# Attention of eight sequences on one core: from two loops of four sequences to one unrolled stream of 128 units, with the shares applied to the weighed values

## The reference

```python
x = x + _L0(x, cond, ...)          # gated recurrence
x = x + _L1(x, cond, ...)          # h = tanh(x Wx + b + h Wh)
x = x + _L2(x, cond, ...)
q, k, v = split(x @ c_attn_w + c_attn_b, 3)
k = concat([cond @ uk_w.T + uk_b, k]);  v = concat([cond @ uv_w.T + uv_b, v])
scores = q k^T / sqrt(32);  scores = where(kj <= qi + 1, scores, -10000.) + mask
out = softmax(scores) @ v
x = x + (out @ c_proj_w + c_proj_b)
```

## Time and profile before

| | |
|---|---|
| median of 3 runs | 4201.73 us (4198.7 to 4204.33) |
| the profiled execution | 4198.98 us, span 4197.3 us |
| recurrences and setup | to 3027.3 us of the span |
| attention loop | 3027.3 to 4197.3 us |
| TensorE busy over the span | 93% |
| VectorE, ScalarE, GpSimd busy | 59%, 25%, 3% |

### The profile page before, as it was taken

One profiled execution on the slowest core, in us unless ns is written; L12 is line 12 of the kernel. 1 busy time (PEld: TensorE's weight loads), 2 busy tenths in 40 slices (PEclk: granted clock), 3 DMA queues, 4 the chain that ended last, 5 costly groups with the idle time before them and its releaser, 6 DMA issues. The chain is left out here.

```text
span 4197.3 us, 167926 instructions
## 1 busy us (share of the span) xinstructions
PE 3891.2 (93%) x75946; PEld 2493.0 (59%) x75946; DVE 2455.8 (59%) x9312; ACT 1057.7 (25%) x3796; POOL 126.9 (3%) x137
## 2 busy tenths in 40 slices
PE   6799999999999999999999999997689888888988
PEld 5577777777666666666666667754444444444444
DVE  3565665665566556566656656653375667557565
ACT  1121111111111111111111111110053454345444
POOL 0000000000000000000000000000000000000000
PEclk9999999999999999999999999999799999999999
DMA  5000000000000000000000000010000000000000
GB/s 182 3 4 4 3 4 3 3 4 3 4 3 3 4 3 3 4 3 3 3 4 3 3 3 3 3 50 15 1 1 11 11 1 11 11 11 1 11 11 11
DMA packets 16600, 44.53 MB, mean 11 GB/s; under 512 B 1474, under 2 KB 1522, under 8 KB 15876
## 3 DMA queue, kind: packets, MB, share of 16 engines
q1 hardware_dynamic: 13572, 27.33, 1.8%
q10 hardware_dynamic: 2304, 6.29, 0.4%
HBM read 25.23 MB, written 8.39 MB: 8 GB/s over the span
## 5 line engine op out<-in xcount | busy, mean ns | idle before, releaser
L181 PE MATMUL bank<-wh,h 128*8 128x256 f32 x16384 | 983.8, 381 | 62.0 <-DVE h L356 31.4
L201 PE MATMUL bank<-wh,h 128*16 128x256 f32 (+1 forms) x17408 | 991.7, 369 | 52.8 <-ACT h L237 50.8
L201 PEld LDWEIGHTS bank<-wh,h 128*16 128x16 f32 (+1 forms) x17408 | 491.1, 97 | 372.0 <-ACT h L237 73.1
L181 PEld LDWEIGHTS bank<-wh,h 128*8 128x8 f32 x16384 | 434.2, 90 | 420.3 <-DVE h L356 50.3
L328 DVE STREAM_TRANSPOSE tp<-bank 128x256 f32<-128x256 f32 x512 | 230.4, 450 | 642.4 <-PE bank L181 642.4
L187 PE MATMUL bank<-wh,h 128*8 128x128 f32 x16384 | 542.3, 273 | 0.0
L187 PEld LDWEIGHTS bank<-wh,h 128*8 128x8 f32 x16384 | 434.7, 90 | 125.3 <-issue 2.0
L250 ACT ACTIVATE gates_sb<-pre_sb 128x32 f32<-128x32 f32 x512 | 118.2, 231 | 1355.6 <-DVE pre_sb L330 1355.6
L225 PE MATMUL bank<-stage,w_qkv 128*32 128x128 f32 x11904 | 382.2, 273 | 0.0
L225 PEld LDWEIGHTS bank<-stage,w_qkv 128*32 128x32 f32 x11904 | 335.7, 110 | 51.2
L269 DVE STREAM_TRANSPOSE tp<-bank 128x256 f32<-128x256 f32 (+1 forms) x544 | 236.1, 434 | 174.0 <-PE bank L201 113.1
(11 more groups left out here) (133 smaller groups left out, 3273.6 us busy)
## 6 DMA issues: line engine op xcount, KB each, us to landing
xrows<-in_x_dram SPq DMA_DIRECT2D x32, 256.0 KB, 3.8
out_dram<-probs SPq DMA_DIRECT2D x32, 256.0 KB, 2.0
w_qkv<-in_L_cond_c_attn_w_dram SPq DMA_DIRECT2D x1, 3072.0 KB, 18.2
wh<-in_L_cond_w_W_dram ACTq DMA_DIRECT2D x4, 512.0 KB, 8.2
w_qkv<-in_L_cond_w_W_dram ACTq DMA_DIRECT2D x4, 512.0 KB, 10.0
wx<-in_L_cond_Wx_dram SPq DMA_DIRECT2D x2, 1024.0 KB, 8.3
wh<-in_L_cond_Wh_dram SPq DMA_DIRECT2D x2, 1024.0 KB, 10.5
wh<-in_L_cond_wh_W_dram ACTq DMA_DIRECT2D x4, 256.0 KB, 8.6
```

The lines of the kernel that those rows point to most:

```text
L181: mm = pe.matmul(mem.ps0[32 * j:32 * j + B, 0:2 * P], h0[:, us, k, ts, :], columns_of(mem.wh0[:, k, 0:3:2, :], j), start=(k == 0), stop=(k ...
L201: mm = pe.matmul(mem.ps12[32 * j:32 * j + B * len(ls), P * l0:P * l1], h12[:, us, k, ts, l0:l1, :].rearrange("p l b -> p (l b)"), columns_ ...
```

## The change

The loop and its barrier go. All 8 x 16 = 128 units are one stream written out, with one numbering of all semaphores from start to end. The parts:

- Probabilities are no longer scaled. The reciprocal of the sums is written over 32 columns per head (`shares`, 128 x 128), transposed by TensorE in the unit's last turn, copied by ScalarE (`shareT`), and VectorE multiplies the weighed values by it as it takes them out of bank 7.
- `weigh` works on one unit instead of a head group: an 8-row matmul for the extras of that query block, then 4 (qc + 1) matmuls of 128 columns. probsT has a buffer per parity of the unit, filled by full banks: a unit has n turns of four transposes and one last turn.
- The last turn of a unit holds the share transpose and the extras matmul, and for qc = 0 also the image scores of the next head group.
- Products are laid over the steps by a table, one in each step (two in step 0 of a sequence): a sequence's own k, q, v and hidden products, the projection of the sequence before (steps 3, 6, 7, 10) and the first products of the next (steps 11 to 15). All go through bank 6. attnT and v have two buffers.
- X is read in place and overwritten by the result's rows; the stores go from X. The copy of X and the mask and image matmuls at a sequence's start go: the mask is loaded broadcast to all rows and as a column, and the image value comes in through a one-row selection in the hidden product (four matmuls instead of three).
- All scores are negated, so maxima become minima and two small VectorE operations of a unit go; the image score is put into place by GpSimd.
- ScalarE copies the first two turns of unit i-2 before the exponentials of unit i-1, the others after them.

```diff
+HEAD_START = [("k", 0), ("q", 0), ("v", 0), ("v", 1), ("v", 2)]
+OWN = {0: [("k", 1), ("v", 3)], 1: [("q", 1)], 2: [("hidden", 0)], 4: [("k", 2)], 5: [("q", 2)],
+       8: [("k", 3)], 9: [("q", 3)]}
+OF_LAST = {3: [("proj", 0)], 6: [("proj", 1)], 7: [("proj", 2)], 10: [("proj", 3)]}
+OF_NEXT = {11: [("v", 0)], 12: [("k", 0)], 13: [("q", 0)], 14: [("v", 1)], 15: [("v", 2)]}
...
 # TensorE
+            def turn(v, first, last):
+                for r in range(qc + 2)[first:last]:
+                    q = ended[v] + r
+                    if q >= 2:
+                        pe.wait_ge(s.turn_kept, q - 1)
...
+                        if r == 0:
+                            pe.wait_ge(s.exps_done, HPG * (v + 1))
...
+                        pe.wait_ge(s.sums_ready, v + 1)
+                        pe.wait_ge(s.extras_in, v + 1)
+                        pe.transpose(bank[:, P:2 * P], mem.shares[:, v % RING, :], mem.ident[:, :])
...
+            def weigh(v):
+                pe.wait_ge(s.turn_kept, ended[v + 1])
...
+                pe.matmul(mem.banks[7][:, cols], mem.v_extra[rows, u % 2, hg * P:(hg + 1) * P],
+                          mem.probs_extra[rows, :], start=True, stop=False, skip_group_check=True)
+                for kc in range(qc + 1):
                     for g in range(HPG):
...
+            for i in range(STEPS):
+                if i < UNITS:
+                    scores(i)
+                if 2 <= i < UNITS + 2:
+                    turn(i - 2, 0, 2)
+                jobs = jobs_of(i) if i < UNITS else []
+                if jobs:
+                    product(*jobs[0])
...
+                if i >= 3:
+                    weigh(i - 3)
+                if 2 <= i < UNITS + 2:
+                    turn(i - 2, 2, None)
+                for job in jobs[1:]:
+                    product(*job)
...
 # ScalarE
+            for i in range(UNITS + 2):
+                if i >= 2:
+                    keep_turn(i - 2, 0, 2)
+                if 1 <= i <= UNITS:
+                    exps(i - 1)
+                if i >= 2:
+                    keep_turn(i - 2, 2, None)
+                if i % PER == 9 and i // PER + 1 < B:
+                    hidden_exps(i // PER + 1)
...
 # VectorE
-                for g in range(HPG):
-                    row = mem.probs[:, slot, g, EXTRAS:EXTRAS + P * (qc + 1)]
-                    nc.vector.tensor_scalar(row, row, mem.scales[:, slot, g:g + 1], None,
-                                            ALU.mult).then_inc(s.probs_ready, 1)
+                nc.vector.reciprocal(mem.shares[:, slot, :].rearrange("p (g c) -> p g c", g=HPG),
+                                     mem.sums[:, slot, :].unsqueeze(2).to_broadcast([P, HPG, HD])).then_inc(s.sums_ready, 1)
...
+                    nc.vector.tensor_tensor(mem.attnT[hg // HG % 2][:, hg % HG, :], mem.banks[7][:, :],
+                                            mem.shareT[:, hg % 2, :], ALU.mult).then_inc(s.weighed_kept, 1)
...
-        with nc.Fori(0, B // BATCHES) as part:
-            attention_batches(nc, mem, sems, a, out, part)
-            clear_signals(nc, mem)
+        attention(nc, mem, sems, a, out)
```

More of the change, by code:

```diff
@@ L619, in _ @@
             dve.wait_ge(s.image_made, 1)
-            dve.wait_ge(s.image_zero, 2)
-            for q, (dst, name) in enumerate(((mem.k_image, "uk_b"), (mem.v_image, "uv_b"))):
-                for hg in range(HG):
-                    for g in range(HPG):
[L625 to L628, removed]
+            dve.wait_ge(s.image_zero, 1)
@@ L634, in attention_batches, with attention @@
-def attention_batches(nc, mem, sems, a, out, part):
+            nc.vector.tensor_scalar(mem.q_bias[:, :], mem.biasT[:, at:at + HG], -HD ** -0.5, None, ALU.mult)
+def attention(nc, mem, sems, a, out):
     s = sems
[L639 to L669, removed]
@@ new lines, in attention, with image_of, probs_blocks, image_scores @@
+    STEPS = UNITS + 3
+    order = [(0, *job) for job in HEAD_START]
+    for i in range(UNITS):
+        order += jobs_of(i)
+    place = {job: n for n, job in enumerate(order)}
+    ended = [0]
+    for i in range(UNITS):
+        ended.append(ended[-1] + unit(i)[2] + 2)
+    def image_of(i):
+        return i // QC + 1 if i % QC == 0 and i // QC + 1 < B * HG else None
+    def probs_blocks(i):
+        u, hg, qc = unit(i)
+        return [(g, k) for g in range(HPG) for k in range(qc + 1)]
+    def image_scores(group):
+        return mem.image_scores[:, group % 2, :]
@@ L835, in _ @@
+            pe.wait_ge(s.weighed_kept, HG * B)
+            for tc in range(QC):
+                project(mem.banks[tc], B - 1, tc, [HG - 1], False).then_inc(s.projected, 1)
         @block.scalar
@@ L848, in keep_turn @@
[L848 to L855 removed]
+                u, hg, qc = unit(i)
+                slot = i % RING
+                act.wait_ge(s.minima_ready, i + 1)
+                act.wait_ge(s.image_in, i + 1)
@@ new lines, in exps, with keep_turn @@
+                nc.scalar.activation(mem.extras[:, slot, 0:EXTRAS * HPG:EXTRAS], mem.neg_max[:, slot, :], ACT.Exp,
+                                     bias=mem.later_max[:, u % 2, qc:qc + 1])
+                for g in range(HPG):
+                    row = mem.probs[qc][:, g, :]
+                    nc.scalar.activation(row, row, ACT.Exp, bias=mem.neg_max[:, slot, g:g + 1], scale=-1.0,
+                                         accum_out=mem.sums[:, slot, g:g + 1]).then_inc(s.exps_done, 1)
+            def keep_turn(v, first, last):
+                u, hg, qc = unit(v)
+                n = HPG * (qc + 1)
+                if first == 0 and v >= 2:
+                    act.wait_ge(s.weighed, v - 1)
+                for r in range(qc + 2)[first:last]:
+                    q = ended[v] + r
+                    act.wait_ge(s.turned, q + 1)
@@ L1033, with extras_in @@
+            def extras_in(i):
+                u, hg, qc = unit(i)
+                pool.wait_ge(s.exps_done, HPG * (i + 1))
+                nc.gpsimd.tensor_copy(mem.extras[:, i % RING, 1:EXTRAS * HPG:EXTRAS], mem.probs[qc][:, :, 0]).then_inc(s.extras_in, 1)
+            for i in range(UNITS + 1):
+                if i < UNITS:
+                    image_in(i)
+                if i:
+                    extras_in(i - 1)
 class Signals:
```

665 lines of the change are left out of this document (324 added, 341 removed).

## The result

In the shared rounds the kernel before took 4200.22 us (median) and the changed kernel 4084.05 us (4076.2 to 4085.6): a ratio of 0.972 with a 95% interval of 0.9703 to 0.9737, 116 us less. The forecast was 4076, the range 4025 to 4150.

The account below looks back on a forecast made before the run. TensorE was taken to bound the kernel. First scores 3055, sequences 985, productless steps 9.5, end steps 2, drains 10 and end 10.3 made 4072, and 4076 with the profile-to-median difference; range 4025 to 4150.

Parts of the forecast that it names:

- drains: Ends of matmul groups before waits: a quarter of the old sequence's 4.9 us kept, 10 us in all.
- the bank wait: In four-block units turn r=4 reuses the bank of r=2 and waits for its copy: 0.4 us, 0 to 1.5.
- the signs that the forecast named: Sequence 126 to 128 us, TensorE over 95% busy, clock near 1.00, scaling gone, VectorE under 75 us, weighing records 0.21.
- those of being wrong: Sequence above 132 us, ScalarE-copy waits over 2 us a group, or share multiply or reciprocal ahead of idle time.
- the way out: From the last projection keep to the span's end: 3.8 us, plus 1 for runs of 512 B.
- The start of the weighing: The 8-row, 128-column matmul that starts each unit's weighing: 0.43 us taken, bounds 0.21 and 0.43.
- the slower rival: Weighing in 128-column pieces does not run four column groups side by side: 0.86 us a block, 205 us, 4281; chance 0.05.
- Head: Before the first scores: mask addends and a strided mask load add 4 us (2 to 8), first scores at 3055.
- the setup: Before attention: half the image matmuls and sixteen VectorE operations go, ten row products come: even, plus or minus 3 us.
- the short runs: At the end, runs of 512 B instead of 2 KB: 1 us added, 0 to 3.
- The clock rival: In the loop TensorE's clock stays low in places, three 6.8 us half-clock stretches a sequence: 82 us, 4158; chance 0.11.
- The wait rival: TensorE's late turns wait for ScalarE's copies if minima come late: 0.5 us a step, 64 us, 4140; chance 0.10.

Follow-up runs that it names:

- e6: Changed kernel with the third turn of four-block units put before the weighing instead of after it: 4073.65 us, ratio 0.9703.
- e10: Changed kernel with VectorE taking the reciprocal of four sums, then spreading it over 128 columns by a copy: 4083.16 us, ratio 0.9718.
- e3: Changed kernel with its 17 products of a sequence in six steps instead of one in each step, same work: 4248.63 us, ratio 1.0122.
- e4: Kernel before without the 512 scalings of the probabilities on VectorE, turns waiting for the scaled extras alone: 4167.99 us, ratio 0.9926.
- e2: Changed kernel with the shares undone, VectorE scaling the probabilities after it keeps the step's product: 4167.81 us, ratio 0.9926.
- e7: e5 plus e6's turn order, and VectorE keeping the first k product before it prepares the mask: 4095.76 us, ratio 0.9752.
- e8: Changed kernel with the image value's 8-row matmul last instead of first in the hidden product: 4072.79 us, ratio 0.9701.
- e9: Changed kernel with e6's early third turn, e8's 8-row matmul last, and the first k product kept before the mask is prepared: 4053.79 us, ratio 0.9646.
- e5: e2 with VectorE scaling unit i-1 before it keeps the step's product, not after: 4104.23 us, ratio 0.9778.

## Why the prediction was right, and its misses

*What bounds, and the sum.* Right. TensorE bounds both kernels and the new time is its own work. Forecast for a sequence 125.8 plus 1.25 of drains (the end of a group of matmuls that a wait lays bare); measured 126.68 without a fall. Forecast for the middle six 762.3 (six times 127.05), measured 761.78. Such closeness has two errors under it: the clock was credited with no loss (it took 1.7 in these six), and the bank wait was taken at 0.4 where the row has 0.24 (four a sequence, 0.6 less). By e6 the two idle terms of the sum seem to be one: without the waits the drains went too. Of the signs that the forecast named, one was missed: VectorE works 77.1 us a sequence, not under 75, by the reciprocal. And of those of being wrong, one is there in small: TensorE waits once 0.5 us for the reciprocal and once 0.8 for the multiply by shares, in the first steps and on the way out.

*Prices not in the trace of before.* The start of the weighing, an 8-row matmul of 128 columns, was bounded by 0.21 and 0.43 and taken at 0.43. It takes 0.42 (3218.65 to 3219.07 above). The 128-column blocks, read from the scan's row at 0.214 for four heads, take 0.79 for three blocks (3219.07 to 3219.86) and 1.01 for four (3106.96 to 3107.97), so 0.214 each and 0.15 once. With that the slower rival, 0.86 a block, falls: the weighing costs what the forecast had it cost. The reciprocal of 128 columns was forecast at 0.3 to 0.6 and took 0.953, outside of that and inside the bounds of 0.28 and 5.7. It didn't matter, and e10 shows it.

*Head.* Forecast first scores at 3055, measured 3059.20. About 3 of the miss lie ahead of the attention, and the change did not make them: the recurrences' last matmuls start 3.7 later (2987.15 and 2990.82), while the setup, forecast as even within 3, is 0.7 shorter. In the head itself 4 were added and it was 5.5 (28.8 against 23.3). Its rows, TensorE and VectorE:

```profile
3030.41 6.43 PE L737 MATMUL bank<-X,w_qkv 128*128 128x512 f32 x8 [5.90 <-PEq L91]
3034.91 0.43 DVE L976 TENSOR_SCALAR neg_far<-mask_all 128x512 f32<-128x512 f32 x1 [5.63 <-DMA mask_col<-in_mask_Bx1x1xS_ff_dram]
3038.78 0.74 DVE L916 TENSOR_SCALAR kT<-bank,biasT 128x512 f32<-128x512 f32 x1
3039.58 5.29 PE L737 MATMUL bank<-X,w_qkv 128*128 128x512 f32 x8 [2.73 <-DVE kT L916]
```

VectorE is idle 5.63 us until the mask's load has landed (3.3 us from its issue), does the addends, and only then keeps k, and TensorE waits 2.73 for that keep. The mechanism was forecast, and the load's time was the unknown. The next product then runs at half clock, 5.29 us.

*From the first scores to the end.* Forecast 1017, measured 1024.7, the largest miss. It is not in the middle (above) but in the first and the last sequence: forecast 254.7 together, measured 112.85 and 150.07, 8.2 more. The step of the forecast that failed is the clock at the ends, taken as full because no step has over 4 us without a product. In each of the two sequences 10.2 us run at 1.2 GHz, which costs 10.2 us of time in all. Half of it begins at the hidden product, half among the steps without a product. One of these steps:

```profile
4028.92 0.93 PE L760 MATMUL bank<-kT,qT 32*128 32x128 f32 x8
4031.10 1.12 PE L784 MATMUL bank<-ident,probs 128*128 128x128 f32 x8 [1.25 <-ACT probs L857]
```

That ScalarE binds there was right, by 1.25 us in this step where about 1 was taken. The way out was shorter than forecast: from the last keep's end to the span's end 4.8 forecast, 3.3 measured (the keep starts at 4079.94 and takes 0.69). The 1 us added for the short runs did not come.

*The sum's two ends.* 4.2 in the head and 7.7 behind it make the span 11.9 longer than forecast; the median lies 0.15 us above the span where 4.5 was added. Left are the 8 us between 4076 and 4084.

*The clock rival* happened in its mechanism but at a seventh of its price: 23.9 half-clock us from the first scores on, so 12 of time, instead of 82. Its three falls a sequence are not there, because the products stand between. e3 shows that the rival was real: take the products away from their places, and 68 of its 82 us come. The Trainium skill ("TensorE: Matmul & The Clock Gate", Part 4: PE-mode transpose) has the rule that transposes do not count as TensorE being busy. The forecast set it aside, and the sequences of 160 transposes of probabilities at clock 1.00 agree with that: beside a product in each step the rule costs nothing that shows. The fall at 3322.7 does not test it, since the 3.40 us ahead of it hold narrow and full matmuls, not transposes.

*The wait rival* did not happen: no row of the middle six names the exponentials or the minima ahead of TensorE. Its ground was misread. The forecast put ScalarE's 129.8 us of waits for the maxima down to VectorE's scaling; e4 leaves the scaling out and has 129.9. What ended these waits, and those for ScalarE's copies, is some part of the new order, and e3 shows only that the spread of the products is needed for it. e2 shows how near a stall is: with the keep and four scalings between the exponentials and the turns, 90 us of waits are back. So the shares are worth little as saved VectorE work (e10 saves another 63 us for nothing). They are worth 84 us where a product's keep would stand ahead of the scaling, and 20 where it would not, because the turns of the probabilities then need nothing of VectorE; only the last turn waits for the reciprocal.

## What to carry to other kernels

When one engine bounds a kernel, write down what it does per step, put the long independent products one to each step between two pieces of a dependent chain, and check the sum by its own work; in this stream the order alone was worth 165 us against the clustered one, more than the whole change. Before an engine is blamed for its load, look whether its operation on the path stands in its queue behind one that waits for the bounding engine: moving it ahead brought 64 of 84 us. And count a short wait at more than its row says: here 0.24 us cost 0.46.

## What the runs showed of the hardware

- TensorE's clock fell to 1.2 GHz with no idle time before: 3.40 of 3.40 us busy with four-column, 8-row and the first full matmuls, then 3.40 us at clock 0.50. Over the middle six sequences there was 1 such fall at the hidden product in the kernel after, 4 in e6, 2 in e10, 3 in e7, and none in e8 and e9, where full matmuls come ahead of the 8-row one. Over all eight sequences it is 3, 6, 3 and 5 against 0 and 0. That is one profile of each kernel: that the order of rows is the cause is likely, not shown, since the placement in time changed as well. It is also not enough by itself: e3 has the 8-row matmul first and no fall there.
- A wait of 0.24 us cost 0.46 (126.68 less 124.83, by four).
- VectorE's reciprocal takes 953 ns for 128 columns and 178 for four, 6.25 ns a column more; a multiply of 512 columns takes 632.

What stays open: the other parts of the change were not tested one by one. These are the weighing by unit, the stream without the copy of X and the mask matmuls, the minima, and ScalarE's copies of two turns ahead of the exponentials, which is a rival for why its copies no longer hold up TensorE. Why e5 has more falls of the clock than the kernel after is not explained, and the 8 us by which e9 beat its expectation were only located (first sequence and clock), not tested one by one.
